# Moving the row normalisation of a graph layer from VectorE to ScalarE

## The chip, the cores and the metric

The kernel runs on one core of one Trainium2 chip. The metric is the device time of one execution in microseconds (us), as the median of several runs.

## The reference

The reference computes one layer on 2500 rows of 1024 numbers. What matters here is its first step and who uses it:

```python
def _layernorm(x, axis=-1, eps=1e-05):
    m = jnp.mean(x, axis=axis, keepdims=True)
    v = jnp.var(x, axis=axis, keepdims=True)
    return (x - m) / jnp.sqrt(v + eps)

xn = _layernorm(x, axis=-1)
x = x + gnn(xn, W, edge_weight, src, dst) + mix(xn[None], Wq, bq, Wk, bk, Wv, bv, weights)[0]
x = x + ffn(_layernorm(x, axis=-1)[None], w_gate, w_up, w_down)[0]
```

The graph part multiplies xn by a 1024x1024 matrix and sums weighted rows over edges. The mixing part projects xn with Wq, Wk and Wv and needs the norms of the whole q and k over all rows. The last part is a feed-forward net with quantised operands.

## The kernel before

The 2500 rows are 20 tiles of 125 rows (one row per partition), held in the tensor X. The change touches stage one alone, the loop over the 20 tiles at the very start. There the kernel normalises each tile, writes its transpose to memory (xnT) for later stages, and adds its share to the left half of the Gram matrix xn^T xn, from which the norms of q and k are worked out later. After tile 19 the same tiles go past once more for the right half of the Gram matrix; then follow the folded projections, the products with the weight matrices, the aggregation over the graph and the feed-forward net, all mostly matmuls.

Each engine has its own program, run in order, and waits on counting semaphores. In stage one:

- VectorE handles pairs of tiles. `row_sums(a, b)` works out mean and variance (L995, L998) into mv. `normalise(a, b)` takes the reciprocal of the deviation (L1004) and normalises each tile in place (L1007). `low_of_rows(n)` (L1012) writes the remainder of X after its rounded part is taken off, into the second half of a slot of `ring`. Tiles 0 and 1 are handled alone, then the order in each turn is: normalise the pair (a, a+1), sums of the next pair, remainder of a, remainder of a+1. In the turn of a = 2, `edge_keys` (L1018 to L1023) stands between.
- ScalarE takes the square root of the variance (`deviations`, L730), writes the rounded part of a tile into the ring (`high_of_rows`, L736), copies the transposed tile out of PSUM (`transposed_rows`, L742) and issues its write to memory (`write_transposed`, L746). Its order in the loop over n is: at even n the deviations of the pair n+2, n+3; then the high part of tile n+1; then the transposed tile n; then the write of n-1. At n = 3 it also moves other transposed data (L771, L774) and issues two transfers.
- TensorE does for each tile n eight transposes (L1421), once the tile is normalised, and then the 12 matmuls of the left Gram part (L1404 to L1406), once its remainder is there. At n = 3 it transposes other data as well, and at n = 4 it waits for ScalarE to have moved these.
- The ring has three slots; the high part of tile n waits for the Gram matmuls of tile n-3. SyncE loads pair p of the rows once the sums of pair p-3 are there. GpSimd clears memory, paced by the Gram matmuls, and later scatters the edges.

Of the kernel before, what the change touches and what calls it, by code (L numbers as in the profile page):

```python
# [28 lines left out]
ALU = mybir.AluOpType  # L29
ACT = mybir.ActivationFunctionType  # L30
AX = mybir.AxisListType

P = 128
# [7 lines left out]
ROWS = 125  # L41
TILES = NODES // ROWS
# [18 lines left out]
NP = TILES // 2  # L61
# [42 lines left out]
def layer_kernel(nc, x, src, dst, edge_weight, W, Wq, bq, Wk, bk, Wv, bv, mix_w, w_gate, w_up, w_down, out):  # L104
# [13 lines left out]
    def zone(label, at, end):  # L118
        cursor[label] = at

        def put(name, shape, dt=F32):
            size = 2 if dt == BF16 else 4
            here = cursor[label]
            cursor[label] = here + (int(np.prod(shape[1:])) * size + 31) // 32 * 32
            assert cursor[label] <= end, (name, cursor[label], end)
            return nc.alloc_sbuf_tensor_at(name, shape, dt, offset=here)
        return put

    small = zone("small", SMALL_AT, KEYS_AT)
# [5 lines left out]
    bias = small("bias", [P, 2, KT, 2])  # L135
    squares = small("squares", [P, 2, KT])
    parts = small("parts", [P, 2, NB + 1])
    mv = small("mv", [P, TILES, 2])
    std = small("std", [P, TILES])
    rstd = small("rstd", [P, TILES])  # L140
    stats = small("stats", [P, GT, 2, 6])
    group_mv = small("group_mv", [P, GT, 2])
    norms = small("norms", [P, 8, 2])
# [32 lines left out]
    X = zone("S1", S_AT, E_AT)("X", [P, TILES, D])  # L176
# [76 lines left out]
    def sem(name):  # L253
        return nc.alloc_semaphore(name)
# [58 lines left out]
    s_rstd = sem("s_rstd")  # L313
# [14 lines left out]
    s_xn = sem("s_xn")  # L328
# [397 lines left out]
    def _(act):  # L726
        def deviations(a, b):
            cols = slice(a, b)
            act.wait_ge(s_st, b)
            nc.scalar.activation(std[0:ROWS, cols], mv[0:ROWS, cols, 1], ACT.Sqrt, bias=eps[0:ROWS, :]).then_inc(s_std, 1)  # L730

        def high_of_rows(n):
            act.wait_ge(s_xn, min(n, TILES - 1) + 1)
            if n >= 3:
                act.wait_ge(s_gm, n - 2)
            nc.scalar.activation(ring[0:ROWS, n % 3, 0, 0:D], X[0:ROWS, n % TILES, :], ACT.Copy).then_inc(s_hi, 1)  # L736
# [18 lines left out]
        nc.scalar.activation(norms[:, 7, 0:1], eps[:, :], ACT.Sqrt)  # L755
        deviations(0, 1)
        high_of_rows(0)
        deviations(1, 2)
        for n in range(TILES):
            if n == 0:  # L760
                high_of_rows(1)
            if n % 2 == 0 and n + 2 < TILES:
                deviations(n + 2, n + 4)
            if n:
                high_of_rows(n + 1)
            transposed_rows(n)
            if n:
                write_transposed(n - 1)
            if n == 3:
                act.wait_ge(s_tr0, 1)  # L770
                nc.scalar.activation(bd[:, :, :], by_block(two_banks(2)), ACT.Copy).then_inc(s_ev0, 1)  # L771
                for q in range(2):
                    act.wait_ge(s_tr0, q + 2)
                    nc.scalar.activation(kT_sb[0:CT, 4 * q:4 * q + 4, :], PS[0:CT, 6 + q, :].rearrange("p (b n) -> p b n", b=4),  # L774
                                         ACT.Copy).then_inc(s_ev0, 1)
                act.wait_ge(s_ev0, 3)
                for q, dram in ((0, key_d), (1, ew_d)):
                    act.dma_start(dram.rearrange("(b c) p -> c b p", c=CT), kT_sb[0:CT, 4 * q:4 * q + 4, :]).then_inc(s_kout, 16)
            if n == 5:
                act.wait_ge(s_tr0, 4)  # L780
                act.wait_ge(s_pad, 4)
                nc.scalar.activation(bias[:, :, :, 0], PS[:, 6, 0:2 * KT].rearrange("p (m j) -> p m j", m=2),
                                     ACT.Copy).then_inc(s_ev0, 1)
# [199 lines left out]
    def _(dve):  # L983
# [5 lines left out]
        def row_sums(a, b):  # L989
            dve.wait_ge((s_x[0], s_second)[a] if a < 2 else s_x[a // 2], 32)  # L990
            if a >= 4:
                dve.wait_ge(s_st, a - 2)
            for t in range(a, b):
                for c in range(2):
                    nc.vector.bn_stats(stats[0:ROWS, t % GT, c, :], X[0:ROWS, t, c * 512:(c + 1) * 512]).then_inc(s_stc, 1)  # L995
            dve.wait_ge(s_stc, 2 * b)
            for t in range(a, b):
                nc.vector.bn_aggr(mv[0:ROWS, t, :], stats[0:ROWS, t % GT, :, :].rearrange("p c n -> p (c n)")).then_inc(s_st, 1)  # L998

        def normalise(a, b):  # L1000
            cols = slice(a, b)
            n = b if b <= 2 else b // 2 + 1
            dve.wait_ge(s_std, n)
            nc.vector.reciprocal(rstd[0:ROWS, cols], std[0:ROWS, cols]).then_inc(s_rstd, 1)  # L1004
            dve.wait_ge(s_rstd, n)
            for t in range(a, b):
                nc.vector.tensor_scalar(X[0:ROWS, t, :], X[0:ROWS, t, :], mv[0:ROWS, t, 0:1], rstd[0:ROWS, t:t + 1],  # L1007
                                        ALU.subtract, ALU.mult).then_inc(s_xn, 1)

        def low_of_rows(n):  # L1010
            dve.wait_ge(s_hi, n + 1)
            nc.vector.tensor_tensor(ring[0:ROWS, n % 3, 1, 0:D], X[0:ROWS, n % TILES, :],  # L1012
                                    ring[0:ROWS, n % 3, 0, 0:D].bitcast(F32), ALU.subtract).then_inc(s_lo, 1)

        def edge_keys():
            dve.wait_ge(s_fill, 4)
            dve.wait_ge(s_edges, 64)
            nc.vector.scalar_tensor_tensor(key[:, 0:FULL], iedge[:, 0, 0:FULL], float(A_PITCH), iedge[:, 1, 0:FULL],  # L1018
                                           ALU.mult, ALU.add).then_inc(s_key, 1)
            nc.vector.scalar_tensor_tensor(key[0:TAIL, FULL:FULL + 1], iedge[0:TAIL, 0, FULL:FULL + 1], float(A_PITCH),  # L1020
                                           iedge[0:TAIL, 1, FULL:FULL + 1], ALU.mult, ALU.add).then_inc(s_key, 1)
            dve.wait_ge(s_key, 2)
            nc.vector.tensor_tensor(away[:, :], away[:, :], key[:, :], ALU.subtract).then_inc(s_key, 1)  # L1023

        row_sums(0, 1)
        normalise(0, 1)
        row_sums(1, 2)
        low_of_rows(0)
        normalise(1, 2)
        low_of_rows(1)  # L1030
        row_sums(2, 4)
        for a in range(2, TILES, 2):
            normalise(a, a + 2)
            if a == 2:
                low_of_rows(2)
                edge_keys()
            if a + 2 < TILES:
                row_sums(a + 2, a + 4)
            for t in range(a + (a == 2), a + 2):
                low_of_rows(t)  # L1040
# [211 lines left out]
        def inverse_deviation(g):  # L1252
            dve.wait_ge(s_std, g + NP + 2)
            nc.vector.reciprocal(rstd[0:ROWS, 0:GT], std[0:ROWS, 0:GT]).then_inc(s_rstd, 1)
            dve.wait_ge(s_rstd, g + NP + 2)

        def quantise_r(g, d):
            largest_r(g, d)
# [31 lines left out]
        with dve.Fori(1, GROUPS) as g:  # L1290
            low_of_sources(0, 0, g * HALF)
            add_z(g - 1)
            low_of_sources(1, 1, g * HALF)
            row_stats(g - 1, ORDER[:2])
            low_of_sources(2, 0, g * HALF + 1)
            row_stats(g - 1, ORDER[2:])
            row_moments(g - 1)
            low_of_sources(3, 1, g * HALF + 1)
            inverse_deviation(g - 1)
            for d in range(GT):  # L1300
                quantise_r(g - 1, d)
                low_of_pair(g, 2 + d)
            with dve.Fori(2 + GT, HALF) as h:
                low_of_pair(g, h)
# [54 lines left out]
        for t in range(1, TILES - GT - 2):  # L1359
            hidden(t // 2, t % 2)  # L1360
            add_down((t - 1) // 2, (t - 1) % 2)
            if t == 2:
                inverse_deviation(GROUPS - 1)
            if t + 1 in ROUNDED_AT:
                largest_r(GROUPS - 1, ROUNDED_AT.index(t + 1))
            if t in ROUNDED_AT:
                round_r(GROUPS - 1, ROUNDED_AT.index(t))
# [348 lines left out]
```

## Time and profile before

| | before |
|---|---|
| median of 3 runs | 1680.78 us (1679.64 to 1681.05) |
| the profiled execution, device time | 1679.44 us |
| its span, first to last instruction | 1677.7 us |
| TensorE busy | 1651.9 us (98%) |
| VectorE busy | 1095.8 us (65%) |
| ScalarE busy | 520.3 us (31%) |
| granted TensorE clock, mean | 0.999 |
| first matmul of the right Gram half | 88.60 us into the span |

The busy times are sums over a program whose stages differ. Stage one fills only the first 88.60 us. The profiled execution took 1.74 us more than its span, and 1.34 us less than the median of the runs.

### The profile page before, as it was taken

How to read it: one execution, taken by the hardware profiler on the slowest of the kernel's cores; microseconds unless marked ns; L12 is line 12 of the kernel's file. 1: busy time of each engine (PE TensorE's matmuls, PEld its weight loads, DVE VectorE, ACT ScalarE, POOL GpSimd, SP SyncE). 2: the span in 40 equal slices, each digit the busy share in tenths (PEclk: the TensorE clock that was granted, in tenths of full speed). 3: DMA queues.
4: the chain of work that ended last, by engine and by line, in shares of the span. 5: the costliest groups of instructions: out<-in, count | busy, mean ns of one | idle time of the engine just before them, and what ended most of it. 6: DMA issues, size and time to landing. Idle time of an engine off the chain costs nothing.

```text
span 1677.7 us, 23245 instructions
## 1 busy us (share of the span) xinstructions
PE 1651.9 (98%) x8036; PEld 1339.5 (80%) x8036; DVE 1095.8 (65%) x2548; ACT 520.3 (31%) x618; POOL 586.5 (35%) x392
## 2 busy tenths in 40 slices
PE   6999999999999999999999999999999999999998
PEld 5899999877888888888877777888777877887665
DVE  7976573577676876656666664476585674764885
ACT  4632310322222111124222222233343333332553
POOL 2012565777776776777677700000000000000000
PEclk9999999999999999999999999999999999999999
DMA  9999977665676756657877747345345345452655
GB/s 306 387 412 331 321 227 245 170 144 118 152 199 162 191 134 149 149 137 196 238 209 197 191 142 210 97 137 143 94 139 143 95 133 141 145 136 61 196 171 171
DMA packets 159147, 307.02 MB, mean 183 GB/s; under 512 B 60386, under 2 KB 95250, under 8 KB 159083
## 3 DMA queue, kind: packets, MB, share of 16 engines
q1 hardware_dynamic: 89447, 226.64, 42.8%
q0 software_dynamic: 61824, 52.62, 15.2%
q10 hardware_dynamic: 7812, 26.97, 5.2%
q8 instruction: 32, 0.52, 0.1%
q14 instruction: 32, 0.26, 0.0%
HBM read 204.92 MB, written 101.24 MB: 182 GB/s over the span
## 4 chain that ended last, share of the span: by engine, by line
PE 95%; DVE 2%; DMA 2%; ACT 1%; issue 0%; ACTq 0%; SPq 0%; DVEq 0%
PE PS L367 24%; PE PS L368 24%; PE PS L366 24%; PE PS L1404 5%; PE PS L1406 5%; PE PS L1405 5%; PE PS L1642 4%; PE PS L1673 2%; PE PS L1469 2%; DMA Aside<-A_dense 1%; PE PS L1421 1%; DVE stats L995 1%; PE PS L1621 1%; PE PS L1384 0%; DVE ring L1012 0%
## 5 line engine op out<-in xcount | busy, mean ns | idle before, releaser
L706 POOL DMA_INDIRECT A_dense<-wtot,cell x336 | 542.6, 1615 | 240.8 <-DMA A_dense<-wtot,cell 141.8
L367 PE MATMUL PS<-SH,AL 125*125 125x512 f32 x784 | 309.6, 395 | 0.0
L368 PE MATMUL PS<-SH,AH 125*125 125x512 f32 x784 | 309.4, 395 | 0.0
L366 PE MATMUL PS<-SL,AH 125*125 125x512 f32 x784 | 308.0, 393 | 1.1 <-DVE AL L1222 1.1
L366 PE MATMUL PS<-WL,xtH 128*125 128x512 f32 x640 | 252.6, 395 | 0.0
L367 PE MATMUL PS<-WH,xtL 128*125 128x512 f32 x640 | 251.7, 393 | 0.0
L368 PE MATMUL PS<-WH,xtH 128*125 128x512 f32 x640 | 251.3, 393 | 0.0
L1220 DVE TENSOR_TENSOR SL<-S,SH 125x1024 fp32r<-125x1024 f32 x98 | 119.9, 1224 | 166.2 <-ACT SH L897 166.1
L897 ACT ACTIVATE SH<-S 125x1024 fp32r (+1 forms) x98 | 104.0, 1061 | 316.8 <-PE PS L368 316.8
L366 PEld LDWEIGHTS PS<-SL,AH 125*125 125x125 f32 x784 | 145.4, 185 | 39.8 <-DVE AL L1222 2.6
L367 PEld LDWEIGHTS PS<-SH,AL 125*125 125x125 f32 x784 | 145.7, 186 | 36.4
L368 PEld LDWEIGHTS PS<-SH,AH 125*125 125x125 f32 x784 | 145.1, 185 | 34.9
L378 DVE SCALAR_TENSOR_TENSOR junk<-keyrow,key,ewrow 128x256 bf16<-128x256 f32 x336 | 149.1, 482 | 0.3 <-issue 0.3
L368 PEld LDWEIGHTS PS<-WH,xtH 128*125 128x125 f32 x640 | 118.5, 185 | 29.2
L366 PEld LDWEIGHTS PS<-WL,xtH 128*125 128x125 f32 x640 | 118.6, 185 | 28.7
L367 PEld LDWEIGHTS PS<-WH,xtL 128*125 128x125 f32 x640 | 118.7, 185 | 28.3
L366 PE MATMUL PS<-TL,xtH 128*125 128x512 f32 x320 | 126.5, 395 | 0.0
L367 PE MATMUL PS<-TH,xtL 128*125 128x512 f32 x320 | 126.5, 395 | 0.0
L368 PE MATMUL PS<-TH,xtH 128*125 128x512 f32 x320 | 126.0, 394 | 0.0
L1120 DVE TENSOR_TENSOR xtL<-xt,xtH 128x1000 fp32r<-128x1000 f32 x60 | 71.7, 1195 | 69.5 <-ACT xtH L828 69.0
L691 POOL DMA_DIRECT2D A_dense<-zeros x40 | 46.8, 1171 | 139.0 <-PE PS L1406 82.5
L1404 PE MATMUL PS<-ring 125*128 125x512 f32 (+4 forms) x260 | 88.9, 342 | 5.6 <-DVE ring L1012 5.6
(189 smaller groups left out, 2546.1 us busy)
## 6 DMA issues: line engine op xcount, KB each, us to landing
A_dense<-zeros POOLq DMA_DIRECT2D x40, 1280.0 KB
xt<-xnT SPq DMA_DIRECT2D x60, 500.0 KB
Araw<-A_dense SPq DMA_DIRECT2D x100, 250.0 KB, 2.7
Aside<-A_dense SPq DMA_DIRECT2D x100, 250.0 KB, 2.9
keyrow<-key_rows SPq DMA_DIRECT2D x42, 512.0 KB
ewrow<-weight_rows SPq DMA_DIRECT2D x42, 512.0 KB
xnT<-XT ACTq DMA_DIRECT2D x20, 500.0 KB, 9.2
zx<-in_x SPq DMA_DIRECT2D x20, 448.0 KB
```

Source lines behind the costliest of these rows:

```text
L366: nc.tensor.matmul(o, lh, rl, start=start, stop=False)
L367: nc.tensor.matmul(o, ll, rh, start=False, stop=False)
L368: return nc.tensor.matmul(o, lh, rh, start=False, stop=stop)
L378: nc.vector.scalar_tensor_tensor(junk[:, slot, 2 * c:2 * c + 2, :].rearrange("p a n -> p (a n)"), row, key[:, col], wrow, ALU.is_equal, AL ...
L706: pool.indirect_dma_start(cells[m], bass.IndirectOffsetOnAxis(cell[:, col:col + 1], 0), wtot[:, col:col + 1], None, compute_op=ALU.add).th ...
L897: nc.scalar.activation(sh, S[0:ROWS, bass.ds(s, 1), :].rearrange("p o n -> p (o n)"), ACT.Copy).then_inc(s_s[i], 1)
L1120: nc.vector.tensor_tensor(xtL[i][:, :, :], xt[:, i], xtH[i][:, :, :].bitcast(F32), ALU.subtract).then_inc(s_xtl[i], 1)
L1220: nc.vector.tensor_tensor(sl, S[0:ROWS, bass.ds(s, 1), :].rearrange("p o n -> p (o n)"), sh.bitcast(F32), ALU.subtract)
L1404: nc.tensor.matmul(o, hi[:, cols], rl, start=first and opens, stop=False, skip_group_check=True)
L1405: nc.tensor.matmul(o, lo[:, cols], rh, start=False, stop=False, skip_group_check=True)
L1406: last = nc.tensor.matmul(o, hi[:, cols], rh, start=False, stop=last_one, skip_group_check=True)
L1642: last = nc.tensor.matmul(PS[0:ROWS, 2 * i + c, :], rqT[:, i, k, 0:ROWS], wT[:, c, :, k * P:(k + 1) * P], start=k == 0, stop=k == KT - 1)
```

## The change

ScalarE now normalises a tile in place, directly ahead of taking its high part, as row times inverse deviation plus a shift. VectorE works out the shift of a pair (minus mean times inverse deviation) in a small instruction after the reciprocal, and no longer touches the rows for this. The semaphore s_rstd now counts two steps for each call.

```diff
+    shift = small("shift", [P, TILES])
...
+        def normalised(t):
+            act.wait_ge(s_rstd, 2 * (t + 1) if t < 2 else 2 * (t // 2 + 2))
+            nc.scalar.activation(X[0:ROWS, t, :], X[0:ROWS, t, :], ACT.Identity, bias=shift[0:ROWS, t:t + 1],
+                                 scale=rstd[0:ROWS, t:t + 1]).then_inc(s_xn, 1)
+
         def high_of_rows(n):
+            if n < TILES:
+                normalised(n)
             act.wait_ge(s_xn, min(n, TILES - 1) + 1)
...
-        def normalise(a, b):
+        def inverse_and_shift(a, b):
             cols = slice(a, b)
             n = b if b <= 2 else b // 2 + 1
             dve.wait_ge(s_std, n)
             nc.vector.reciprocal(rstd[0:ROWS, cols], std[0:ROWS, cols]).then_inc(s_rstd, 1)
-            dve.wait_ge(s_rstd, n)
-            for t in range(a, b):
-                nc.vector.tensor_scalar(X[0:ROWS, t, :], X[0:ROWS, t, :], mv[0:ROWS, t, 0:1], rstd[0:ROWS, t:t + 1],
-                                        ALU.subtract, ALU.mult).then_inc(s_xn, 1)
+            dve.wait_ge(s_rstd, 2 * n - 1)
+            nc.vector.scalar_tensor_tensor(shift[0:ROWS, cols], mv[0:ROWS, cols, 0], -1.0, rstd[0:ROWS, cols],
+                                           ALU.mult, ALU.mult).then_inc(s_rstd, 1)
...
-            dve.wait_ge(s_rstd, g + NP + 2)
+            dve.wait_ge(s_rstd, g + 2 * NP + 3)
```

The four calls of `normalise` in VectorE's program become calls of `inverse_and_shift` at the same places. The last line only adapts the count of the same semaphore in a later stage.

## Rows read from the trace of the kernel before

**Rows 1.** The page's first part: busy us (share of the span) and instructions of each engine.

```profile
PE 1651.9 (98%) x8036; PEld 1339.5 (80%) x8036; DVE 1095.8 (65%) x2548; ACT 520.3 (31%) x618; POOL 586.5 (35%) x392
```

**Rows 2.** The page's fourth part, the chain that ended last, by engine.

```profile
PE 95%; DVE 2%; DMA 2%; ACT 1%; issue 0%; ACTq 0%; SPq 0%; DVEq 0%
```

**Rows 3.** TensorE's waits from 86 us to the end: total us, times, longest us.

```profile
PE PS L1655 <- ACT hq L955: 3.5, 2, 2.2
PE PS L366 <- DVE AL L1222: 1.1, 2, 0.8
...
```

**Rows 4.** VectorE's timeline, one pair of stage one: start us, length us, instruction [idle before].

```profile
48.76 1.23 DVE L1012 TENSOR_TENSOR ring<-X,ring 125x1024 fp32r<-125x1024 f32 x1 [0.22 <-ACT ring L736]
49.90 0.16 DVE L1004 RECIPROCAL rstd<-std 125x2 f32<-125x2 f32 x1
50.10 1.54 DVE L1007 TENSOR_SCALAR X<-X,mv,rstd 125x1024 f32<-125x1024 f32 x2
51.55 2.46 DVE L995 BATCH_NORM_STATS2 stats<-X 125x6 f32<-125x512 f32 x4
54.05 0.28 DVE L998 BATCH_NORM_AGGREGATE mv<-stats 125x2 f32<-125x12 f32 x2
54.24 1.17 DVE L1012 TENSOR_TENSOR ring<-X,ring 125x1024 fp32r<-125x1024 f32 x1
55.64 1.23 DVE L1012 TENSOR_TENSOR ring<-X,ring 125x1024 fp32r<-125x1024 f32 x1 [0.22 <-ACT ring L736]
```

**Rows 5.** ScalarE's timeline over the same stretch.

```profile
54.36 0.29 ACT L730 ACTIVATE std<-mv,eps 125x2 f32<-125x2 f32 x1 [1.15 <-DVE mv L998]
54.56 1.04 ACT L736 ACTIVATE ring<-X 125x1024 fp32r<-125x1024 f32 x1
55.51 1.01 ACT L742 ACTIVATE XT<-PS 128x1000 f32<-128x1000 f32 x1
...
57.82 1.06 ACT L736 ACTIVATE ring<-X 125x1024 fp32r<-125x1024 f32 x1 [1.30 <-DVE X L1007]
```

**Rows 6.** TensorE's timeline: Gram of tile 6; transposes of 18, 19; first right-half matmul.

```profile
41.71 0.50 PE L1404 MATMUL PS<-ring 125*128 125x512 f32 x1 [1.18 <-DVE ring L1012]
...
81.99 1.02 PE L1421 MATMUL PS<-ident,X 125*128 125x125 f32 x8
...
85.30 1.01 PE L1421 MATMUL PS<-ident,X 125*128 125x125 f32 x8
...
88.60 0.40 PE L1404 MATMUL PS<-ring 125*128 125x512 f32 x1
```

**Rows 7.** Timelines of VectorE and ScalarE in the first 36 us.

```profile
12.36 1.23 DVE L1012 TENSOR_TENSOR ring<-X,ring 125x1024 fp32r<-125x1024 f32 x1 [1.13 <-ACT ring L736]
...
18.78 1.23 DVE L1012 TENSOR_TENSOR ring<-X,ring 125x1024 fp32r<-125x1024 f32 x1 [0.40 <-ACT ring L736]
...
20.94 2.47 DVE L995 BATCH_NORM_STATS2 stats<-X 125x6 f32<-125x512 f32 x4
...
25.03 1.23 DVE L1012 TENSOR_TENSOR ring<-X,ring 125x1024 fp32r<-125x1024 f32 x1 [1.31 <-ACT ring L736]
...
28.18 0.99 ACT L742 ACTIVATE XT<-PS 128x1000 f32<-128x1000 f32 x1
...
33.72 0.29 ACT L730 ACTIVATE std<-mv,eps 125x2 f32<-125x2 f32 x1 [1.36 <-issue]
```

**Rows 8.** Groups by line: busy us, mean ns | idle before; an Identity with bias, a small VectorE product.

```profile
L913 ACT ACTIVATE rq<-rc,neg_round 125x1024 f32 x16 | 18.2, 1136 | 0.0
L393 DVE SCALAR_TENSOR_TENSOR dup<-dup,away 128x8 f32<-128x8 f32 x42 | 7.1, 168 | 4.7
```

**Rows 9.** ScalarE's timeline where a square root is followed by an Identity.

```profile
1567.44 1.28 ACT L908 ACT_TABLE_LOAD   x1
...
1568.96 0.72 ACT L955 ACTIVATE hq<-hid,neg_round 125x512 bf16<-125x512 f32 x1
```

**Rows 10.** GpSimd's edge scatter, line 706: duration ns, first and last start us.

```profile
L706 POOL DMA_INDIRECT A_dense<-wtot,cell x336: 1533/1543/2513, 165.6 to 965.6; - x168
```

More of the change, by code:

```diff
@@ L1025, in _ @@
         row_sums(0, 1)
-        normalise(0, 1)
+        inverse_and_shift(0, 1)
         row_sums(1, 2)
         low_of_rows(0)
-        normalise(1, 2)
+        inverse_and_shift(1, 2)
         low_of_rows(1)
@@ L1032, in _ @@
         for a in range(2, TILES, 2):
-            normalise(a, a + 2)
+            inverse_and_shift(a, a + 2)
             if a == 2:
```

## The prediction, made before the changed kernel ran

> **What bounds the kernel now.** I read the page first: TensorE is busy for 98% of the span [rows 1], and 95% of the chain that ended last is TensorE [rows 2]. So whatever TensorE loses anywhere is lost in the end, unless it waits later for something that comes at a fixed time. Next I read TensorE's waits behind stage one: the longest one after 86 us is 2.2 us [rows 3], and those waits are for ScalarE and VectorE work that itself follows from matmuls. The one long job that runs on its own beside TensorE is the scatter of the edges; its last issue is at 965.6 us [rows 10], and it starts only when stage one has let it, so it moves with the delay. The question is thus by how much the first right-half matmul moves from 88.60 us [rows 6].
>
> Then I read stage one itself. In its steady part a pair takes 6.88 us (remainder of an odd tile at 48.76, the next at 55.64 [rows 4]). VectorE is busy for nearly all of it: 1.23 + 0.16 + 1.54 + 2.46 + 0.28 + 1.17, less small overlaps, and 0.22 idle. TensorE alone would take 85.30 - 81.99 = 3.31 us per tile, 6.62 per pair [rows 6]. So VectorE is the limit here, by 0.26 us per pair, and TensorE is right behind. ScalarE has about 4.2 us of work per pair (0.29, two of 1.06, two of 1.0 [rows 5]) and waits for the rest.
>
> **The change, priced.** VectorE loses the two normalising instructions, 1.54 us per pair [rows 4], and gains one small product. Its price is near 168 ns, that of another small product [rows 8]; I take 0.16 (bounds: 0.14 and 0.30), and 0.04 for the wait on its own result (0.16 from 49.90, the next at 50.10 [rows 4]). ScalarE gains 20 full-width instructions with two pointer operands. The trace shows none such. An activation of 1024 columns with plain numbers takes 1.06 [rows 5], one with a bias pointer 1.136 [rows 8]; the step of 0.08 taken twice gives 1.22, and I take 1.23. Bounds: 1.06 (the pointers cost nothing) and 1.32 (a pointer for scale costs twice that for bias).
>
> The Trainium skill, "ScalarE: Activation LUTs", section "What ACT_TABLE_LOAD costs", gives 186 ns plus 0.833 ns per column and about 93 ns for each pointer operand: 1.225 us as an estimate from that page. The sum would be the same by it; no row shows an instruction with two.
>
> What matters more than the price is that the high part now stands behind ScalarE's own result. In the trace two instructions that don't depend overlap by 0.10 us (54.56 + 1.04, the next at 55.51 [rows 5]); a dependent one starts some 0.04 after the end of the other. So normalise plus high part take 1.23 + 0.04 + 1.06 = 2.33 us. Before, the high part alone was on ScalarE, and VectorE did both tiles in one go, long before they were wanted. Behind the waiting normalise stand, in ScalarE's queue, the high part, the transposed tile (which TensorE needs for its bank), its transfer to memory, and the deviations of the next pair.
>
> *The start, step by step* (a hop between engines counted as 0.04, remainder 1.21, next one on VectorE 0.07 before its end):
> - Tile 0: reciprocal ends 6.95, shift 7.15, normalise 7.19 to 8.42, high to 9.52, remainder to 10.77. Tile 1: shift 11.06, normalise 11.10 to 12.33, high to 13.43; its remainder starts at 13.47, against 12.36 [rows 7]: +1.1.
> - Sums of the pair (2, 3) follow and end at 17.40; root to 17.73; the copy of transposed tile 0 (0.99) is next in ScalarE's queue, so normalise(2) is 18.52 to 19.75, high to 20.85, remainder from 20.89, against 18.78 [rows 7]: +2.1.
> - Here is the worst place. normalise(3) stands behind the root of pair (4, 5), which needs its sums, which VectorE does after the remainder of tile 2 and the edge keys. Remainder and keys took 20.94 - 18.78 = 2.16 [rows 7]; now they end near 23.0, the sums at 25.80, the root at 26.13, normalise(3) 27.26, high 28.36, remainder from 28.40, against 25.03 [rows 7]: +3.4.
> - Remainder of 3 to 29.61, reciprocal and shift to 29.90, normalise(4) to 31.17, high to 32.27, transposed tile 3 from 32.17, against 28.18 [rows 7]. From there to the next root the queue is as before (the extra transposes, the three copies, two transfers): 33.72 - 28.18 = 5.54 [rows 7], so it comes at 37.7. normalise(5) 39.12, high 40.22, remainder to 41.47, shift 41.76, normalise(6) 43.03, high 44.13. VectorE meanwhile does the sums of (8, 9), to 44.48, then the remainder of 6 to 45.62. The Gram part of tile 6 starts at 45.66, against 41.71 [rows 6]: +3.95.
>
> *The steady part* is then a ring through both engines. From the end of one odd high part: remainder, reciprocal, shift and hops 0.04 + 1.21 - 0.07 + 0.16 + 0.04 + 0.16 + 0.04 = 1.58; normalise and high of the even tile 2.33; transposed tile and root 0.98 (0.99 and 0.29 less three overlaps of 0.10); normalise and high of the odd tile 2.33. That is 7.22 us per pair, against 6.88 now and 6.62 that TensorE needs. VectorE's sums are covered: they end some 0.5 us before the root can start; if they were late, the ring would grow by that. The high part of 7 ends at 47.53; five rings on, that of 17 ends at 83.63; then 1.58 + 2.33 + 0.04 + 1.21 + 0.04 to the Gram part of tile 18 at 88.83. TensorE does it (2.53, that is 3.31 less 0.78 for transposes), transposes 19 (0.78), does its Gram part (2.53), and begins the right half at 94.67, against 88.60 [rows 6]: +6.07. The same steps and prices walked through for the kernel before come out at 89.1 instead of 88.60, that is a bit long; I take off 0.2 and keep **+5.9 us**.
>
> In parts: the start up to tile 6 gives +3.95, five rings at +0.34 give +1.7, the last pair the rest. The term that hangs most on the unknown price: each 0.01 us on a normalise costs about 0.19 us in all.
>
> After the right half begins nothing of the change is left, and the later stages follow 5.9 us later. The two extra counts of the semaphore cost nothing. The sum against the profiled execution: 1679.44 + 5.9 = 1685.3. That execution lies 1.34 below the median; against the median of the runs it is 1680.78 + 5.9 = **1686.7 us**, 0.35% slower. A measurement of this kernel can tell about 0.2% (3.4 us) from no change.
>
> **Rivals.**
> - *The pointers cost nothing (1.06).* Then the ring is 6.88, the same as now, and only the longer start is left: by the same steps +2.8, 1683.6 us, which is within 0.2%. It stops being so at a price near 1.10. For it: the 1.06 of all plain activations. Against: the 1.136 with one pointer [rows 8]. Chance 0.12.
> - *VectorE's relief decides (the other side).* VectorE had 6.66 of 6.88 us busy; with 1.54 less the pair could go at TensorE's 6.62, which would save 0.26 us on each of six pairs: 1.6 us, 1679.2 us. For more than 0.2% the stalls of the start would have to go as well. It decides only if normalise(t) is done before its place in the queue matters, that is if ScalarE's ring stays under 6.62, for which a normalise would have to cost under 0.93 us; at the price of a plain activation it is already over. Chance 0.07, of which 0.04 below by over 0.2%.
> - *The tables alternate.* If Identity with pointers wanted another function table than the square root, each of 11 roots would bring two loads of 1.28 us [rows 9]: 28 us, near 1709. Against: the Identity with a bias after the root of 1567.44 comes without a load between [rows 9], where it is the root that had to load. The Trainium skill, "ScalarE: Activation LUTs", section "Table sets: the hidden batching unit", has identity in every set; by that rule there is no load, and the trace agrees. Chance 0.03.
> - *Dearer hops or a dearer normalise.* If a dependent start on ScalarE and the hops cost 0.08 instead of 0.04, the same walk gives +8.4; with a normalise of 1.32, +7.6. Some 1689.0 us. Chance 0.08.
>
> The forecast itself keeps 0.70. Its own spread and the bounds above give the range 1683.2 to 1690.0. Slower by over 0.2%: the forecast, the tables and the dear hops, 0.81; within 0.2%: the free pointers and part of the relief, 0.15; faster 0.04.
>
> **What the changed profile would show.** ScalarE's group for the normalise 20 times at 1.2 us; the pair in the steady part at 7.2 us on VectorE's remainders of odd tiles, with over 1 us of idle time per pair ahead of them that names ScalarE; the root of the fourth pair near 37.7; the Gram part of tile 6 near 45.5; the right half starting near 94.5; the rest of the span shifted as a block. The prediction is wrong if the normalise costs much less than 1.2, if the high part starts without waiting for its whole input, or if a later wait takes up the delay: then TensorE's idle time after 95 us would be less than before.

## The result and the profile after

The changed kernel takes 1686.47 us (median of 6 runs, 1685.1 to 1687.89), beside 1680.18 us for 6 runs of the kernel before: ratio 1.0033, 95% interval 1.0022 to 1.0044. Run again later beside other runs of the kernel before it took 1686.0 against 1681.15, ratio 1.0027 (1.0018 to 1.0036). So it is slower by 0.3%, 5 to 6 us. The forecast was 1686.7 us, +5.9. The profiled execution of the changed kernel, 1687.89 us, was the slowest of its six; that of the kernel before, 1679.44, was below its median. Differences between the two profiles, 6.98 us at the right half among them, are therefore a little larger than those of the medians.

The page of the kernel after, its first part (busy us and share by engine) and its fourth (the chain that ended last), answer to [rows 1] and [rows 2]:

```profile
PE 1655.6 (98%) x8036; PEld 1345.3 (80%) x8036; DVE 1082.1 (64%) x2539; ACT 543.1 (32%) x638; POOL 585.1 (35%) x392
...
PE 91%; ACT 3%; DVE 3%; DMA 2%; issue 1%; ACTq 0%; SPq 0%; DVEq 0%
```

VectorE lost 14 us of work, ScalarE gained 23. TensorE has the same matmuls, but its share of the last chain fell from 95% to 91%: the missing part is now ScalarE's, VectorE's and "issue", time for which the profile shows no cause. That is no measure of the loss, since 4% of the span is 67 us: it says that in stage one the chain which ended last now runs through these engines instead of TensorE. Where it went is seen in the timelines. ScalarE over one pair of the steady part (start us, length us, [idle before it <- what ended that]), to be held against [rows 5]:

```profile
60.40 0.28 ACT L731 ACTIVATE std<-mv,eps 125x2 f32<-125x2 f32 x1
60.59 1.23 ACT L735 ACTIVATE X<-X,shift,rstd 125x1024 f32<-125x1024 f32 x1
61.85 1.06 ACT L744 ACTIVATE ring<-X 125x1024 fp32r<-125x1024 f32 x1
...
62.82 0.98 ACT L750 ACTIVATE XT<-PS 128x1000 f32<-128x1000 f32 x1
64.48 1.25 ACT L735 ACTIVATE X<-X,shift,rstd 125x1024 f32<-125x1024 f32 x1 [0.68 <-DVE shift L1014]
65.76 1.06 ACT L744 ACTIVATE ring<-X 125x1024 fp32r<-125x1024 f32 x1
```

And VectorE over the same pair, to be held against [rows 4]:

```profile
62.95 1.23 DVE L1019 TENSOR_TENSOR ring<-X,ring 125x1024 fp32r<-125x1024 f32 x1 [1.91 <-ACT ring L744]
64.09 0.16 DVE L1012 RECIPROCAL rstd<-std 125x2 f32<-125x2 f32 x1
64.28 0.16 DVE L1014 SCALAR_TENSOR_TENSOR shift<-mv,rstd 125x2 f32<-125x2 f32 x1
...
70.14 1.23 DVE L1019 TENSOR_TENSOR ring<-X,ring 125x1024 fp32r<-125x1024 f32 x1 [1.90 <-ACT ring L744]
```

Read the two together. The high part ends at 62.91, the remainder starts at 62.95, the reciprocal at 64.09, the shift at 64.28, and ScalarE, idle for 0.68 us, normalises the next tile at 64.48. From there to the high part of the odd tile ScalarE is without a gap. That is the ring, and it takes 70.14 - 62.95 = 7.19 us. VectorE now waits 1.9 us ahead of each odd remainder, where it waited 0.22 before. The group of the normalise (by line, busy us, mean ns | idle before):

```profile
L735 ACT ACTIVATE X<-X,shift,rstd 125x1024 f32<-125x1024 f32 x20 | 24.7, 1237 | 7.2 <-DVE shift L1014 7.2
```

The start, ScalarE's and VectorE's timelines, against [rows 7]:

```profile
25.93 1.23 ACT L735 ACTIVATE X<-X,shift,rstd 125x1024 f32<-125x1024 f32 x1
...
38.23 0.29 ACT L731 ACTIVATE std<-mv,eps 125x2 f32<-125x2 f32 x1 [1.70 <-issue]
...
45.91 0.19 ACT L790 ACTIVATE bias<-PS 128x16 f32<-128x16 f32 x1 [0.38 <-PE PS L1448]
45.99 0.29 ACT L731 ACTIVATE std<-mv,eps 125x2 f32<-125x2 f32 x1
```

```profile
28.28 1.23 DVE L1019 TENSOR_TENSOR ring<-X,ring 125x1024 fp32r<-125x1024 f32 x1 [2.58 <-ACT ring L744]
```

TensorE's timeline gives the two marks of [rows 6], the Gram part of tile 6 and the first matmul of the right half (41.71 and 88.60 before):

```profile
46.64 0.48 PE L1411 MATMUL PS<-ring 125*128 125x512 f32 x1
...
95.58 0.40 PE L1411 MATMUL PS<-ring 125*128 125x512 f32 x1
```

The right half starts 6.98 us later. Its waits from 92 us on (total us, times, longest us) answer to [rows 3], whose first row comes back as it was:

```profile
PE PS L1662 <- ACT hq L963: 3.5, 2, 2.2
PE PS L367 <- DVE AL L1229: 2.0, 2, 1.9
```

From the right half to the end it is 1686.1 - 95.58 = 1590.5 us, before 1677.7 - 88.60 = 1589.1. So the change is in stage one; the 1.4 us behind it is of the size by which runs of one kernel differ (1685.1 to 1687.89), and 0.9 of it is seen in the second of these waits.

One thing was not in the forecast: TensorE's clock (columns: stretch, us, busy, granted clock, share and rate of the transfers; 1.00 is 2.4 GHz, 0.50 would be 1.2 GHz throughout). The kernel after:

```profile
22.00:26.00 4.00, 3.96 (x12) 0.57 1.02 255
26.00:30.00 4.00, 1.81 (x11) 0.89 1.05 339
30.00:34.00 4.00, 4.00 (x17) 0.68 1.02 315
...
20.00:40.00 20.00, 15.24 (x76) 0.83 1.03 293
```

and the kernel before:

```profile
20.00:40.00 20.00, 15.72 (x95) 1.00 1.04 355
```

### The profile page after: what moved, and what is told of

Same layout as the page of the kernel before. It is cut to its first block, busy times and chain, and to the rows that moved or that the text cites. A ratio compares the mean times of both kernels' runs of the same rounds, so it can differ in the third digit from the quotient of the medians.

```text
span 1686.1 us, 23260 instructions
## 1 busy us (share of the span) xinstructions
PE 1655.6 (98%) x8036; PEld 1345.3 (80%) x8036; DVE 1082.1 (64%) x2539; ACT 543.1 (32%) x638; POOL 585.1 (35%) x392
## 4 chain that ended last, share of the span: by engine, by line
PE 91%; ACT 3%; DVE 3%; DMA 2%; issue 1%; ACTq 0%; SPq 0%; DVEq 0%
PE PS L368 23%; PE PS L367 23%; PE PS L369 23%; PE PS L1411 4%; PE PS L1412 4%; PE PS L1413 4%; PE PS L1649 4%; PE PS L1680 2%; DMA Aside<-A_dense 2%; PE PS L1476 2%; ACT X L735 1%; DVE ring L1019 1%; ACT ring L744 1%; PE PS L1628 1%; PE PS L1391 0%
```

## The experiments

All are timed beside the kernel before on the same chip. "Right half" is the start of its first matmul in the profiled execution: 88.60 us before, 95.58 after. It comes from one execution of each kernel, the medians from 7 to 11.

How far one execution's start scatters is seen in two kernels below that have the same order up to tile 5 as the kernel before (the second of 2, and 5, whose extra product is small): there the remainder of tile 5 starts at 35.78 and 36.39 us, in the kernel before at 35.00. In the two profiles of the changed kernel it starts at 40.78 and 41.34. So a difference of under 1 us at the right half says little.

**1. What the price of the instruction is worth.** The two pointer operands are taken away, every wait stays. The kernel leaves out the factor and the shift, so its rows are not normalised; only its time is used.

```diff
-            nc.scalar.activation(X[0:ROWS, t, :], X[0:ROWS, t, :], ACT.Identity, bias=shift[0:ROWS, t:t + 1],
-                                 scale=rstd[0:ROWS, t:t + 1]).then_inc(s_xn, 1)
+            nc.scalar.activation(X[0:ROWS, t, :], X[0:ROWS, t, :], ACT.Copy).then_inc(s_xn, 1)
```

> This kernel leaves out the factor and the shift: ScalarE's instruction on the rows is a plain copy in place, so each of the 20 costs 1.06 us instead of 1.24, while every wait stays. Theory one (the time goes into a chain through ScalarE's queue and VectorE's remainder, on which each normalise lies): 7 of them in the start, 10 in the five steady pairs and 2 at the end, 19 times 0.18 is 3.4 us, so the right half starts near 92.1 instead of 95.6, a steady pair takes 6.86 instead of 7.20, and the run is near +2.9 against the kernel before. Rival (TensorE's clock at its lower level in the start costs the time, not the chain): the right half stays near 95.

Measured: 1682.87 us, ratio 1.0018 (1.0009 to 1.0028). The instruction fell to 1.05 us, as its group shows:

```profile
L756 ACT ACTIVATE X<-X 125x1024 f32<-125x1024 f32 x20 | 21.0, 1051 | 7.3 <-DVE shift L1040 7.3
```

Pairs took 6.83 us (68.64 - 61.81 on VectorE's odd remainders), the right half began at 93.28. So the ring follows the price of both normalises in it, 7.20 to 6.83. The right half came 1.2 us later than expected: the remainder of tile 3 started 0.4 us sooner than in the changed kernel (27.88), but the Gram part of tile 3, at the lower clock here too (0.83 from 20 to 40 us), took 33.80 - 29.16 = 4.64 us to the next transposes instead of 3.91, and the remainder of tile 5 started at 40.77, in the changed kernel at 40.78. This execution, 1688.17 us, was the slowest of ten, in part by a later wait of TensorE for VectorE (3.9 us, where the changed kernel has 2.0); only its stage one is read here. Even a normalise at the price of a copy would have left the kernel slower: this was the first rival, and its time was foretold as 1683.6.

**2. The start alone and the rest alone.** Which engine normalises a tile is made a list; in one kernel ScalarE has tiles 0 to 5 (shown), in the other all from 6 on, `tuple(range(6, TILES))`.

```diff
+ON_ACT = tuple(range(6))
...
-            if n < TILES:
+            if n in ON_ACT:
                 normalised(n)
...
+            for t in on_dve:
+                nc.vector.tensor_scalar(X[0:ROWS, t, :], X[0:ROWS, t, :], mv[0:ROWS, t, 0:1], rstd[0:ROWS, t:t + 1],
+                                        ALU.subtract, ALU.mult).then_inc(s_rstd, 1)
```

> Only tiles 0 to 5 are normalised on ScalarE, the rest on VectorE as before. Theory one: the start costs what it did in the changed kernel, the Gram part of tile 6 begins near 46 instead of 41.7, and from there a pair takes 6.88 as in the kernel before: right half near 93.0 (+4.4), the run +4.4 or less by what the pairs can catch up. Rival (the cost is ScalarE's load in all of stage one): under a third of 6.3 us, about +2.

> Tiles 0 to 5 are normalised on VectorE as in the kernel before, the other 14 on ScalarE. Theory one: the start is that of the kernel before, the Gram part of tile 6 near 41.7 to 42.5, then 7.20 per pair: right half near 90.6 (+2.0), the run +2.0. Also TensorE's clock stays at its upper level in the first 40 us. Rival (ScalarE's load): over two thirds of 6.3 us, about +4.3.

Measured: the first six 1684.44 us, ratio 1.0030 (1.0019 to 1.0042), right half at 95.31, pairs 6.88. From six on: 1681.29 us, ratio 1.0010 (0.9995 to 1.0025), right half at 90.57, pairs 7.20, clock 1.00 from 20 to 40 us. TensorE's timeline of the second:

```profile
90.57 0.40 PE L1438 MATMUL PS<-ring 125*128 125x512 f32 x1
```

Six of twenty tiles cost nearly the whole sum (1.0030, beside 1.0033 and 1.0027 for all twenty); that excludes ScalarE's load as the cause. The other fourteen came to +2.0 at the right half, as expected, but in part by luck: 0.78 of it stood there at the remainder of tile 5 (35.78 against 35.00), before ScalarE had normalised a tile. The first part was dearer than expected (+6.7 at the right half, not +4.4). Its start was 0.7 us longer than in the changed kernel (remainder of tile 5 at 41.51, not 40.78), and I had taken the mark at tile 6 over from a kernel in which VectorE no longer normalises there: from the remainder of tile 5 (41.51) the VectorE order needs another 6.71 us to the Gram part of tile 6 (48.22), as in the kernel before (35.00 to 41.71), and not the 5.86 of the changed kernel.

The two parts add up to 8.7 us, not to 6.98. Most of the excess, 0.73 + 0.78, lies ahead of the remainder of tile 5 and is the scatter of the two starts. One gain is in the second part and in the changed kernel alike: where ScalarE normalises, VectorE has less to do behind the last sums, and from the remainder of tile 17 to the right half it takes 95.58 - 84.54 = 11.0 us instead of 12.3 (88.60 - 76.28).

**3. The place in ScalarE's queue.** The changed kernel, with the root of the next pair behind the high part.

```diff
-            if n % 2 == 0 and n + 2 < TILES:
-                deviations(n + 2, n + 4)
+            if n == 0:
+                deviations(2, 4)
             if n:
                 high_of_rows(n + 1)
+            if n and n % 2 == 0 and n + 2 < TILES:
+                deviations(n + 2, n + 4)
```

> As the changed kernel, but from n = 2 on ScalarE takes the square root of the next pair behind the high part of tile n+1, not ahead of its normalise. Theory one: normalise of tile 3 no longer stands behind the sums of pair (4, 5); the remainder of tile 3 starts near 25.7 instead of 28.28, and this 2.6 us stays; in the steady part the root no longer lies on the chain, 7.0 instead of 7.20 per pair, 1 us in five. Right half near 92.0, the run near +2.7. Rival (ScalarE's load decides, its work is the same): right half stays near 95.6, run +6.3.

Measured: 1681.22 us, ratio 1.0006 (0.9997 to 1.0016); right half at 90.55. VectorE's timeline, the remainders of tiles 3 and 5 and two of the steady part:

```profile
25.55 1.17 DVE L1048 TENSOR_TENSOR ring<-X,ring 125x1024 fp32r<-125x1024 f32 x1
...
36.87 1.23 DVE L1048 TENSOR_TENSOR ring<-X,ring 125x1024 fp32r<-125x1024 f32 x1 [5.68 <-ACT ring L765]
...
65.48 1.23 DVE L1048 TENSOR_TENSOR ring<-X,ring 125x1024 fp32r<-125x1024 f32 x1 [1.72 <-ACT ring L765]
...
72.50 1.23 DVE L1048 TENSOR_TENSOR ring<-X,ring 125x1024 fp32r<-125x1024 f32 x1 [1.72 <-ACT ring L765]
```

The remainder of tile 3 starts at 25.55, 2.7 us sooner; a pair takes 7.02. ScalarE does the very same 20 instructions of 1.24 us as in the changed kernel, and most of the loss is gone: the interval of what is left includes none. More came back than I had expected (5.0 at the right half, not 3.6): at tile 5 the gain had grown from 2.73 to 40.78 - 36.87 = 3.91. Of the 1.18 us, 0.35 came between the remainder of tile 3 and the copies at n = 3, 0.64 because the second of the two transfers took 0.36 us to issue instead of 1.00, and 0.19 because the root no longer stands between these transfers and the normalise of tile 5. The issue took 0.32 to 1.22 us over all the runs, and what sets it was not tried, so some of this gain need not belong to the order.

**4. Opening the ring.** All tiles on ScalarE in the old order, but VectorE takes reciprocal and shift ahead of the odd remainder.

```diff
+        inverse_and_shift(2, 4)
         for a in range(2, TILES, 2):
-            inverse_and_shift(a, a + 2)
...
-            for t in range(a + (a == 2), a + 2):
-                low_of_rows(t)
+            if a > 2:
+                low_of_rows(a)
+            if a >= 2 and a + 2 < TILES:
+                inverse_and_shift(a + 2, a + 4)
+            low_of_rows(a + 1)
...
```

> As the changed kernel (all tiles on ScalarE), but VectorE takes the reciprocal and the shift of the next pair ahead of the remainder of the odd tile, not behind it. Theory one (a ring through both engines: high part, remainder, reciprocal, shift, normalise): the ring opens and ScalarE's idle 0.67 us ahead of each even normalise is gone; a pair is then limited by TensorE's 6.62 (ScalarE's own work is 7.20 - 0.67 = 6.53): five pairs by 0.58 and some 1.4 in the start, right half near 91.2 instead of 95.6, the run near +2.6 against the kernel before. Rival (ScalarE's load itself is the limit): pairs stay at 7.2 and the right half near 95.

Measured: 1682.23 us, ratio 1.0008 (0.9998 to 1.0017); right half at 92.52. VectorE's remainders, one pair:

```profile
61.52 1.23 DVE L1046 TENSOR_TENSOR ring<-X,ring 125x1024 fp32r<-125x1024 f32 x1 [1.23 <-ACT ring L765]
...
68.03 1.23 DVE L1046 TENSOR_TENSOR ring<-X,ring 125x1024 fp32r<-125x1024 f32 x1 [1.23 <-ACT ring L765]
```

They are 6.51 us apart, ScalarE's own work without the 0.67 of waiting; TensorE follows in 6.62. So in the changed kernel it was the ring, not ScalarE's load, that held the pairs at 7.2. The start won nothing (remainder of tile 5 at 41.53, clock 0.83 from 20 to 40 us), where 1.4 us was expected; that is the 1.3 us to the expected 91.2.

**5. The small product alone.** The kernel before, with the shift worked out on VectorE beside its own normalise and used by nobody.

> The kernel before with the shift worked out on VectorE in addition and used by nobody. Theory one: VectorE limits a pair in the kernel before, so the small product adds its own 0.16 us less an overlap, near 0.1 to 0.2 per pair: pairs near 7.0 instead of 6.88, right half near 89.5, the run within 1 us of the kernel before. Rival (the small product and its wait are a large part of the change's 6.3 us): +2 or more.

Measured: 1680.55 us, ratio 0.9995 (0.9985 to 1.0004); pairs 6.95 (71.14 - 64.19), right half at 90.43. The product costs 0.07 per pair where VectorE limits. The right half is 1.8 us later than in the kernel before, of which the pairs explain 0.4; the rest lies in the start of this execution (remainder of tile 5 at 36.39 instead of 35.00, clock 0.91 from 20 to 40 us), and the median shows no loss.

**6. Half the tiles on ScalarE.** Odd tiles from 7 on are normalised on ScalarE, all others on VectorE; from the pair (6, 7) on reciprocal, even normalise and shift stand ahead of the odd remainder (the edit is that of 4 with the list of 2).

> From tile 6 on only the odd tiles are normalised on ScalarE, the even ones on VectorE, all earlier ones on VectorE; from the pair (6, 7) on reciprocal, shift and the even normalise stand ahead of the remainder of the odd tile. Theory one: start as in the kernel before, then neither VectorE (6.88 - 0.77 and a shift, about 6.2) nor ScalarE (about 5.5) limits a pair, TensorE does with 6.62: right half 1.6 us earlier than before, near 87.0, the run near -1.5. Rival (TensorE cannot use it, its waits in the start decide all): no change, 88.6.

> The kernel of odd_on_scalar, unchanged, to settle whether it beats the kernel before. Theory one: TensorE limits the pairs from tile 8 on (6.62 instead of 6.88), the run 1.5 to 2.5 us faster than before, ratio 0.9985 to 0.999. Rival (its first result was scatter of the runs): ratio 1.000.

Measured: 1678.22 us, ratio 0.9985 (0.9975 to 0.9995), right half at 88.72; again 1679.34 us, ratio 0.9988 (0.9979 to 0.9997), right half at 89.11. By the medians it beats the kernel before by 0.1%, 2 to 3 us, and both intervals end just below 1. The profiles don't show the gain: neither right half reaches the expected 87.0, and both lie behind the 88.60 of the kernel before. At the remainder of tile 5 these executions are 1.5 and 1.1 us later than that one (their clock was 0.91 from 20 to 40 us), and ScalarE waited 7.6 and 5.9 us in all for writes whose buffers it wanted again (1.6 in the kernel before). In the first, TensorE also stood still between the halves, which was not followed up:

```profile
87.94 0.33 PE L1445 MATMUL PS<-ring 125*128 125x386 f32 x1
88.72 0.47 PE L1443 MATMUL PS<-ring 125*128 125x512 f32 x1 [0.45 <-issue]
```

In its steady part the transposes are 3.31 and 3.30 us apart, TensorE's own time per tile, so there neither of the two other engines limits:

```profile
61.52 1.02 PE L1460 MATMUL PS<-ident,X 125*128 125x125 f32 x8
...
64.83 1.01 PE L1460 MATMUL PS<-ident,X 125*128 125x125 f32 x8
...
68.13 1.02 PE L1460 MATMUL PS<-ident,X 125*128 125x125 f32 x8
```

**7. The order of 3 in the kernel before.** No tile on ScalarE; the edit of 3.

> The kernel before (all tiles on VectorE) with one change of order on ScalarE: from n = 2 on the square root of the next pair comes behind the high part of tile n+1. Theory one: the high part of tile 3 no longer stands behind the sums of pair (4, 5): its remainder starts at 23.7 instead of 25.03; and VectorE's 0.22 us of idle time per pair goes, 6.66 instead of 6.88 in five or six pairs. Right half near 86.2, the run near -2.4, a version that beats both. Rival (VectorE would wait for the root instead): pairs stay at 6.88 and only the start's 1.3 us is won.

Measured: 1680.1 us, ratio 0.9992 (0.9983 to 1.0002); right half at 90.84, not 86.2. The start did as expected (remainder of tile 3 at 23.56, Gram part of tile 6 at 39.71, 2.0 us sooner than before). But transfers were late. VectorE's timeline, waiting for rows, and ScalarE's:

```profile
27.43 2.47 DVE L1026 BATCH_NORM_STATS2 stats<-X 125x6 f32<-125x512 f32 x4 [1.05 <-DMA X<-in_x]
```

```profile
48.24 1.01 ACT L771 ACTIVATE XT<-PS 128x1000 f32<-128x1000 f32 x1 [5.43 <-DMA xnT<-XT]
```

ScalarE stood for 5.43 us for the write of tile 3, whose buffer it wanted again; that write took 16.1 us from issue to landing, and in the kernel before the longest in the same stretch took 12.2. This execution, 1683.54 us, was the slowest of ten, and others took 1677.1. So in this execution the expectation failed on a resource that I had not counted; whether the median lost its gain in the same way, one profile can't say.

**8. The same with the crowd thinned out.** GpSimd's clearing of memory, one strip per four tiles in stage one, is held back.

```diff
-                pool.wait_ge(s_gm, min(4 * r, TILES))
+                pool.wait_ge(s_gm, TILES)
```

> The kernel of vector_root_behind, with GpSimd's clearing of memory from the second strip on held back until the left Gram half is done (it was one strip for each four tiles). Theory one: in stage one the transfers are near their limit, and what vector_root_behind lost (5.4 us of ScalarE waiting for the write of tile 3, 1.1 for rows) came from this crowd; without the strips the waits for transfers vanish and the right half starts near 86.2 instead of 90.8. Its run: the scatter starts some microseconds later but ended 20 us before it was needed, so near -2.4. Rival (the waits come from the queue of row loads, not from the strips): right half stays near 90; or the late clearing is paid where the aggregation starts.

Measured: 1677.62 us, ratio 0.9977 (0.9967 to 0.9987). TensorE's timeline:

```profile
86.01 0.40 PE L1440 MATMUL PS<-ring 125*128 125x512 f32 x1
```

The right half begins at 86.01, expected was 86.2, and from 15 us to there no engine waits for a row or a write. The scatter, whose rows give duration ns and first and last start, runs later than in [rows 10] by 20 us at its first issue and by 6 at its last, and nobody notices:

```profile
L728 POOL DMA_INDIRECT A_dense<-wtot,cell x336: 1533/1542/2562, 185.7 to 971.8; - x168
```

This version beats both kernels, with every tile normalised on VectorE. That the strips were what made the write of 7 late is likely, not shown: each version has one profile, that of 7 from its slowest execution, and the two ratios to the kernel before, 0.9992 (0.9983 to 1.0002) and 0.9977 (0.9967 to 0.9987), still touch.

**9. The changed kernel again.**

> The changed kernel once more, unchanged, beside the next two on one chip, to have its place next to the versions of mixed order. Theory one: near +6 against the kernel before, right half near 95, normalise 1.24 us, pairs 7.2. TensorE's clock again falls to its lower level at the Gram parts of tiles 2 and 3, behind the long idle stretches of the start, and the part of tile 3 then takes near 3.9 us instead of 2.96. Rival (the clock in the profile before was an accident of one execution): clock 1.0 in the first 40 us, and the right half near 94.6.

Measured: 1686.0 us, as told above; right half at 96.09, and over 20 to 40 us:

```profile
20.00:40.00 20.00, 16.46 (x75) 0.74 1.03 292
```

The lower clock was no accident of one execution. The normalise took 1.236 us, a pair 7.20, and the Gram part of tile 3 33.81 - 29.71 = 4.10 us to the next transposes.

## Why the prediction was right, step by step

- *Who decides.* "Whatever TensorE loses anywhere is lost in the end": right. Stage one moved the right half by 6.98 us, and no later wait took any of it up.
- *The price.* Forecast 1.23 us, taken as two steps of 0.08 over a plain activation; measured 1.237. The estimate of 1.225 from the Trainium skill ("ScalarE: Activation LUTs", section "What ACT_TABLE_LOAD costs") lies 0.012 below the measured mean: the trace agrees. The shift took 0.16, as taken; where VectorE limits it costs less (experiment 5).
- *The ring.* Forecast 7.22 us, measured 7.19 to 7.20; its opening (experiment 4) and its shortening by the root (experiment 3) and by the price (experiment 1) gave close to what they should: 6.51 on VectorE with TensorE at its 6.62, 7.02 and 6.83. The terms were right one by one: the gap from high part to normalise was 0.68 idle behind 0.89 of the transposed tile, 1.57 against 1.58.
- *The start.* The remainder of tile 3 came at 28.28 (forecast 28.40), and the place in the queue behind the root was the reason (experiment 3). Behind it three things were missing. The root of the pair (6, 7) came at 38.23 instead of 37.7: the Gram part of tile 3 took 33.47 - 29.56 = 3.91 us to the next transposes, in the kernel before 29.27 - 26.31 = 2.96, since TensorE ran at its lower clock, of which 0.30 was left over at ScalarE's copies; and the two transfers took 0.34 longer to issue. Then the root of (8, 9) came at 45.99 instead of 45.0: it stands behind the copy of the transposed bias (45.91), which waits for TensorE, which waits for transposed tile 5. In the kernel before this wait lay beside another and cost nothing; I had left it out, and it is 0.46 us.
- *The sum.* By the steps +6.07 at the right half, measured +6.98: +0.5 for clock and issue, +0.46 for the bias, the ring within 0.1. The 0.2 that I took off had no ground here. That the medians (+6.3, then +4.9) lie around the forecast +5.9 is in part luck: the walk put the right half at 94.67, and it came 0.9 and 1.4 us later in the two profiled executions. The other side of the difference was off as well: the 88.60 that it starts from is one execution, and the start of that one was 0.8 and 1.4 us quicker than in the two later ones of the same order.
- *The rivals.* Free pointers: excluded by 1.237, and worth what was said when made so. VectorE's relief: it was real, 14 us of work less, and stood idle; by the medians it pays a little where the other engine keeps slack (experiment 6). Tables: in stage one only the load of the kernel's first root, and 13 in all, as before. Dearer hops: the starts of dependent instructions were 0.03 to 0.04 after the end, as taken.

## What to carry to other kernels

Before work is moved to an engine that looks idle, walk its queue: what a moved instruction stands behind, and what then stands behind it. Here an engine with a third of its time busy lost 5 to 6 us for the kernel, because the moved step lay behind a square root that waited for the other engine, and closed a ring through both. Changing the order won back most of that without moving any work (experiment 3). Once the order is right, the next limit decides what is left to win; here late transfers are the likely one (7 and 8).

## What was not expected of the hardware

TensorE's clock fell in the start. From 20 to 40 us it was 1.00 in the kernel before, with the first six tiles on VectorE and ScalarE after them (2), and in experiments 7 and 8; 0.83 and 0.74 in the changed kernel, 0.83 in experiments 1, 4 and the first of 2, and 0.91 in 3, 5 and 6. In the changed kernel it was 0.57 from 22 to 26 us, behind 2.33 us without work ahead of the transposes of tile 2 and 1.27 ahead of its Gram part. In the kernel before the two waits are 0.78 and 1.28, and the clock stays at 1.00. Both are rows of TensorE's timeline, of the kernel after:

```profile
19.69 1.07 PE L1428 MATMUL PS<-ident,X 125*128 125x125 f32 x8 [2.33 <-ACT X L735]
22.04 0.59 PE L1411 MATMUL PS<-ring 125*128 125x512 f32 x1 [1.27 <-DVE ring L1019]
```

and of the kernel before:

```profile
17.72 1.07 PE L1421 MATMUL PS<-ident,X 125*128 125x125 f32 x8 [0.78 <-DVE X L1007]
20.07 0.50 PE L1404 MATMUL PS<-ring 125*128 125x512 f32 x1 [1.28 <-DVE ring L1012]
```

In the changed kernel the matmuls behind these waits ran at a lower clock, so the waits cost more than their own length. But the length of the waits doesn't decide it alone. The kernel before waited 2.69 us ahead of the Gram part of tile 3 and stayed at 1.00; the first kernel of experiment 6 waited 2.68 at the same place and was at 0.57 from 28 to 32 us. The row of the kernel before, then that of experiment 6 and its stretch:

```profile
26.31 0.50 PE L1404 MATMUL PS<-ring 125*128 125x512 f32 x1 [2.69 <-DVE ring L1012]
```

```profile
26.92 0.50 PE L1443 MATMUL PS<-ring 125*128 125x512 f32 x1 [2.68 <-DVE ring L1046]
...
28.00:32.00 4.00, 4.00 (x18) 0.57 1.01 332
```

What decides it was not found, and what the fall costs by itself was not tried. The 0.91 of experiments 5 and 6, whose first tiles are normalised on VectorE, shows that it isn't bound to this change alone.

The other thing is how much the transfers can matter in stage one. An order that made the engines 2 us quicker met waits of up to 5.4 us in its profiled execution (7); with the strips of unrelated clearing, 1.3 MB each, held back, these were gone, and the ratio to the kernel before went from 0.9992 to 0.9977. The busy share of the transfers doesn't tell the two apart: from 15 to 60 us it is 1.03 in the kernel before, in 7 and in 8. What differs is what they moved, 361, 363 and 329 GB/s.
